# A four-layer graph network that streams its adjacency matrix: six fours in the last upper pair, states turned in couples, four steps moved

## The reference

```python
h = relu(layernorm(x));  x = x + adj @ (h * keep / 0.9)               # layer 0
h = relu(layernorm(x));  deg = clip(rowsum(adj) + 1, 1)               # layer 1
z = concat([h, (adj @ h + h) / deg]) @ W1 + b1
x = x + relu(z) / norm(relu(z))
h = relu(layernorm(x));  a = adj + I;  d = rowsum(a) ** -0.5          # layer 2
x = x + ((d[:, None] * a * d[None, :]) @ h) @ W2
h = relu(layernorm(x))                                                # layer 3
x = x + concat([h, (adj @ h) / (rowsum(adj) + 1)]) @ W3.T
```

## Time and profile before

| | |
|---|---|
| median of 3 runs | 1855.67 us |
| profiled execution | 1858.4 us |
| its span, first to last instruction | 1856.6 us |
| TensorE busy | 1806.5 us (97%) |
| VectorE busy | 1461.4 us (79%) |
| ScalarE, GpSimd busy | 102.1 us, 9.1 us |
| HBM read | 673.3 MB, 365 GB/s over the span |
| mean granted TensorE clock | 0.998 |

### The profile page before, as it was taken

How to read it: one execution, slowest core, us unless ns; L and a number is a source line. 1 busy time by engine, 2 the same in 40 slices (tenths; PEclk the granted TensorE clock), 3 DMA queues, 4 the chain that set the end, 5 groups by cost and what they waited for, 6 DMA issues and landing times.

```text
span 1856.6 us, 21067 instructions
## 1 busy us (share of the span) xinstructions
PE 1806.5 (97%) x8392; PEld 624.2 (34%) x8392; DVE 1461.4 (79%) x1529; ACT 102.1 (6%) x270; POOL 9.1 (0%) x23
## 2 busy tenths in 40 slices
PE   5899999999999999999999999999999999999998
PEld 1223333333333333333333333333333333333333
DVE  8989899999997765669888664678878787877754
ACT  0000000000000000100000000111000000000000
POOL 0000000000000000000000000000000000000000
PEclk9999999999999999999999999999999999999999
DMA  9999999999988878298797798499899999999995
GB/s 384 421 421 421 421 421 421 421 421 421 416 333 319 318 282 298 70 408 329 293 393 317 302 365 333 167 366 420 347 422 374 421 383 421 421 393 421 421 421 236
DMA packets 96047, 676.79 MB, mean 365 GB/s; under 512 B 11216, under 2 KB 13264, under 8 KB 14288
## 3 DMA queue, kind: packets, MB, share of 16 engines
q1 hardware_dynamic: 93024, 673.23, 89.1%
q10 hardware_dynamic: 2928, 2.23, 0.4%
HBM read 673.32 MB, written 2.10 MB: 364 GB/s over the span
## 4 chain that ended last, share of the span: by engine, by line
PE 88%; DMA 7%; DVE 4%; issue 0%; SPq 0%; ACT 0%; DVEq 0%
PE acc L776 43%; DMA ring<-stream_in 7%; PE acc L976 5%; PE acc L950 5%; PE DEG L932 4%; PE acc L806 3%; PE HT L776 2%; PE acc L963 2%; PE Z L832 2%; PE acc L1162 2%; PE DEG L1174 2%; PE acc L1079 2%; PE acc L1055 2%; PE acc L1069 2%; PE acc L1110 1%; PE acc L1117 1%
## 5 line engine op out<-in xcount | busy, mean ns | idle before, releaser
L776 PE MATMUL acc<-ring,states 128*64 128x512 f32 x3984 | 901.7, 595 | 33.7 <-DMA ring<-stream_in 29.1
L776 PEld LDWEIGHTS acc<-ring,states 128*64 128x64 f32 x3984 | 286.8, 137 | 583.3 <-issue 553.3
L1579 DVE TENSOR_TENSOR row_sum<-row_sum,ring 128x2048 f32<-128x2048 f32 x194 | 444.6, 2292 | 14.7 <-DMA ring<-stream_in 9.7
L1703 DVE TENSOR_TENSOR ring<-row_totals,ring 128x2048 f32<-128x2048 f32 x27 | 61.8, 2289 | 56.1 <-PE DEG L934 55.9
L932 PE MATMUL DEG<-ring,states 128*64 128x512 f32 x216 | 99.2, 602 | 3.6 <-DMA ring<-stream_in 3.6
L950 PE MATMUL acc<-row_totals,row_sum 128*64 128x512 f32 x216 | 97.3, 593 | 2.7 <-DVE row_sum L1695 2.7
L934 PE MATMUL DEG<-ring,states 128*64 128x512 f32 x216 | 99.3, 603 | 0.0
L978 PE MATMUL acc<-ring,states 128*64 128x512 f32 x216 | 97.7, 595 | 0.0
L976 PE MATMUL acc<-ring,row_sum 128*64 128x512 f32 x216 | 97.7, 595 | 0.0
L952 PE MATMUL acc<-ring,row_sum 128*64 128x512 f32 x216 | 97.3, 593 | 0.0
L776 PE MATMUL acc<-diag,states 128*64 128x512 f32 x336 | 91.1, 594 | 0.6 <-DMA diag<-stream_in 0.6
(11 more groups left out here) (207 smaller groups left out, 2087.0 us busy)
## 6 DMA issues: line engine op xcount, KB each, us to landing
ring<-stream_in SPq DMA_DIRECT2D x610, 1024.0 KB, 12.5
diag<-stream_in SPq DMA_DIRECT2D x28, 1024.0 KB, 13.2
x<-x_in SPq DMA_DIRECT2D x4, 512.0 KB, 7.0
y<-u_in SPq DMA_DIRECT2D x4, 512.0 KB, 8.9
x_out<-x ACTq DMA_DIRECT2D x16, 128.0 KB, 6.7
below<-w_in ACTq DMA_DIRECT2D x6, 16.0 KB, 5.7
bias<-b_in ACTq DMA_DIRECT2D x1, 32.0 KB, 10.0
```

Source lines behind the costliest of these rows:

```text
L776: return nc.tensor.matmul(half_of(bank, half), h[layer % 2][:, J], moving, start=start, stop=stop)
L1579: nc.vector.tensor_tensor(row_sum[:, :], before, slot(key)[:, :], ALU.add).then_inc(unit_summed, 1 if count > 1 else 2)
```

## The change

1. The last upper pair (2, 1) gets two more fours, on sources (7, 6) and (5, 4), in place of four `plain_both`. Their formed states go into the diagonal slots that the first two couples held.
2. `turn_own` takes several rows: it does their transposes one behind the other, into alternate halves of HT. Rows 14 and 13, and 12 and 11, are turned together; each later pair's two rows are turned right behind the `finish` of the pair before (`close_and_turn`); in the down stage rows b-2 and b-1 behind `finish(c)`, at the end of the pair.
3. Row 15's layer-1 diagonal product, its turn and `finish(1, 15)` come one head step sooner.
4. `cover(15)` goes into the upper head, ahead of `SECOND_D[3]`. `cover(11)` goes from pair 1 to the end, `cover(6)` from the end to pair 4, ahead of `plain` 3. The loads and the let-go order follow.
5. `add_one_again` of the first head diagonal goes ahead of `gather_1(0)`.
6. In the down stage the first sum of each pair's second four is formed sooner (`first_down_form(p, 1)`), behind `end_layer_2(b - 1)`.

```diff
+LAST_SOURCE_PAIRS = [(7, 6), (5, 4)]
 FOURS = [[sp for sp in SOURCE_PAIRS if sp[1] > hi] for hi, lo in PAIRS]
+FOURS[-1] += LAST_SOURCE_PAIRS
+SOURCE_PAIRS += LAST_SOURCE_PAIRS
...
-    [("cover", 15), ("cover", 13), ("four", 0), ("near", 0), ("four", 1), ("plain", 11)],
-    [("cover", 12), ("four", 0), ("four", 1), ("near", 1), ("four", 2), ("cover", 11), ("plain", 9)],
+    [("cover", 13), ("four", 0), ("near", 0), ("four", 1), ("plain", 11)],
+    [("cover", 12), ("four", 0), ("four", 1), ("near", 1), ("four", 2), ("plain", 9)],
...
-    [("cover", 7), ("four", 0), ("four", 1), ("near", 4), ("four", 2), ("four", 3), ("plain", 7), ("plain", 6),
-     ("plain", 5), ("plain", 4), ("plain", 3)],
+    [("cover", 7), ("four", 0), ("four", 1), ("near", 4), ("four", 2), ("four", 3), ("four", 4), ("four", 5),
+     ("cover", 6), ("plain", 3)],
...
-COVER_AT_END = [6, 5, 4, 3, 2, 1]
+COVER_AT_END = [11, 5, 4, 3, 2, 1]
...
-        out += [("sums", p, 0), ("fourth", p, 0), ("turn", 2 * p), ("rest", p, 0)]
-        out += groups(min(p, 2)) + [("turn", 2 * p + 1)] + ([("group", ("own", b - 1))] if p else [])
+        out += [("sums", p, 0), ("fourth", p, 0)] + ([] if p else [("turn", 0, 1)])
+        out += [("rest", p, 0)] + groups(min(p, 2)) + ([("group", ("own", b - 1))] if p else [])
...
-        out += [("rest", p, last), ("near", p)] + groups(1) + [("group", ("near", p)), ("finish", c)]
-    out += groups(1) + [("turn", ROWS - 4)] + groups(1) + [("turn", ROWS - 3)] + groups(len(waiting))
-    return out + [("group", ("own", LAST)), ("turn", ROWS - 2)]
+        out += [("rest", p, last), ("near", p)] + groups(1) + [("group", ("near", p)), ("finish", c), ("turn", b - 2, b - 1)]
+    return out + groups(len(waiting)) + [("group", ("own", LAST))]
...
+            def turn_own(layer, *rows_of_layer):
+                first = TURNS.index((layer, rows_of_layer[0]))
+                if first > 0:
+                    pe.wait_ge(hT_copied, first)
...
+                for n, b in enumerate(rows_of_layer, first):
+                    pe.wait_ge(scaled_ready, n + 1)
+                    for k in range(2):
+                        mm_t = nc.tensor.transpose(turned(n)[:, k * P:(k + 1) * P], scaled[n % 2][:, k * P:(k + 1) * P],
+                                                   ident[:, :])
+                mm_t.then_inc(hT_done, len(rows_of_layer))
...
+            def close_and_turn(p):
+                if p > 0:
+                    finish(1, PAIRS[p - 1][1])
+                turn_own(1, *PAIRS[p])
...
             head_first(2, FIRST_A[1])
-            head_first(2, FIRST_A[2])
             pe.wait_ge(diag_plus_one, ROWS)
...
-            head_first(2, FIRST_C[0], behind=lambda: finish(1, LAST))
+            head_first(2, FIRST_A[2], behind=lambda: finish(1, LAST))
+            head_first(2, FIRST_C[0])
...
             head_second(2, SECOND_D[2], behind=lambda: finish(1, 12))
+            pe.wait_ge(*gathered(1, LAST))
+            cover(LAST)
             head_second(2, SECOND_D[3], behind=lambda: finish(1, 11))
             head_second(2, SECOND_D[4])
-            pe.wait_ge(*gathered(1, LAST))
...
-            end_layer_1(15, lambda: gather_1(14), lambda: gather_1(13))
+            end_layer_1(15, None, lambda: gather_1(14))
+            gather_1(13)
...
+                if len(FOURS[p]) > 4:
+                    for n in range(len(SOURCE_PAIRS) - len(LAST_SOURCE_PAIRS), len(SOURCE_PAIRS)):
+                        form_states(n)
+                    first_form(p, 4)
+                    third_form(p, 4)
+                    last_forms(p, 4)
+                    first_form(p, 5)
+                    third_form(p, 5)
+                    last_forms(p, 5)
                 end_layer_1(before_lo)
...
+            add_one_again(ADDED[0])
             gather_1(0)
-            for r in ADDED[:HEAD]:
+            for r in ADDED[1:HEAD]:
...
                     end_layer_2(b - 1)
+                    first_down_form(p, 1)
                     fold_up_to(GROUPS.index(("own", b - 1)) - 1)
...
+                scale_own(3, b - 2)
+                scale_own(3, b - 1)
                 gather_low_and_parts(p)
```

More of the change, by code:

```diff
@@ L273, in units_let_go @@
         out[at:at + len(ended)] = ended
+        if phase == 2:
+            out.insert(at + 2 * STEPS_AHEAD_OF_COVER, out.pop(at + len(ended)))
     down = down_let_go()
@@ L416, in formed, with turned @@
             at = n % 2 * 4 * FEATS + (t - 1) * FEATS
-            return diag[n // 2][:, at:at + FEATS].rearrange("p (k f) -> p k f", f=F)
+            return diag[n // 2 % 2][:, at:at + FEATS].rearrange("p (k f) -> p k f", f=F)
+        def turned(n):
+            return HT[:, n % 2 * 2 * P:(n % 2 + 1) * 2 * P]
         def down(name):
@@ L616, in copy_hT @@
             def copy_hT(layer, b):
-                act.wait_ge(hT_done, TURNS.index((layer, b)) + 1)
+                n = TURNS.index((layer, b))
+                act.wait_ge(hT_done, n + 1)
                 by_parity = own_y(b, 1).rearrange("p (k l n) -> p l k n", k=2, l=2)
                 for parity in range(2):
-                    turned = HT[parity * F:(parity + 1) * F, 0:2 * P].rearrange("p (k n) -> p k n", k=2)
-                    done = nc.scalar.copy(by_parity[:, parity], turned)
+                    half = turned(n)[parity * F:(parity + 1) * F, :].rearrange("p (k n) -> p k n", k=2)
+                    done = nc.scalar.copy(by_parity[:, parity], half)
                 done.then_inc(hT_copied, 1)
@@ L1045, in cover, with four_even @@
                 both_at_once((2, 0, g), BANK_UP[0], g == LAST, g == 1)
-            def four_even(p, i, after_first=None, after_second=None):
+            def four_even(p, i, after_first=None):
                 (hi, lo), (s1, s2) = PAIRS[p], FOURS[p][i]
@@ L1074, in four_even @@
                 four.then_inc(unit_freed, 1)
-                if after_second is not None:
-                    after_second()
                 pe.wait_ge(unit_formed, 3 * n + 2)
@@ L1224, in _ @@
                         turn_degrees()
-                    if b == LAST and g in (12, 13):
-                        turn_own(1, 26 - g)
+                    if b == LAST and g == 13:
+                        turn_own(1, 14, 13)
                 pe.wait_ge(*diag_arrived(1, b))
@@ L1279, in _ @@
                             pe.wait_ge(part_copied, PARTS.index((2, 11)) + 1)
-                        four_even(p, 0, after_first=(lambda: finish(1, PAIRS[p - 1][1])) if p else None,
-                                  after_second=lambda: turn_own(1, hi))
-                        turn_own(1, lo)
-                    elif kind == "four" and n % 2 == 0:
+                        four_even(p, 0, after_first=lambda: close_and_turn(p))
+                    elif kind == "four" and n == 2:
                         four_even(p, n, after_first=lambda: near_diagonal(p))
@@ L1286, in _ @@
                             turn_own(1, 0)
+                    elif kind == "four" and n % 2 == 0:
+                        four_even(p, n)
                     elif kind == "four":
@@ L1331, in _ @@
                 elif kind == "turn":
-                    turn_own(3, what)
+                    turn_own(3, *step[1:])
                 elif what[0] == "near":
@@ L1677, in early_forms, with third_down_form @@
                 dve.wait_ge(down_formed, 4 * n + 1)
+            def third_down_form(p, i):
+                n = DOWN_BEFORE[p] + i
+                a21, a22, a11, a12 = down_four(p, i)
                 dve.wait_ge(*loaded(a11))
@@ L1681, in early_forms @@
                 dve.wait_ge(down_formed, 4 * n + 2)
+            def early_forms(p, i):
+                first_down_form(p, i)
+                third_down_form(p, i)
             def state_forms(p, i):
@@ L1796, in _ @@
                 end_layer_1(before_hi, begun=True)
-                for n in range(FORMED_BY_GPSIMD, len(SOURCE_PAIRS)):
+                for n in range(FORMED_BY_GPSIMD, len(SOURCE_PAIRS) - len(LAST_SOURCE_PAIRS)):
                     if SOURCE_PAIRS[n][1] == before_hi:
@@ L1832, in _ @@
                     fold_up_to(GROUPS.index(("near", p - 1)) + 1)
-                scale_own(3, 2 * p)
-                scale_own(3, 2 * p + 1)
+                if p == 0:
+                    scale_own(3, 0)
+                    scale_own(3, 1)
                 second_form(p, 0)
@@ L1839, in _ @@
                     end_layer_2(b - 1)
+                    first_down_form(p, 1)
                     fold_up_to(GROUPS.index(("own", b - 1)) - 1)
                 for i in range(1, last):
-                    early_forms(p, i)
+                    if i == 1:
+                        third_down_form(p, i)
+                    else:
+                        early_forms(p, i)
                     state_forms(p, i)
```

32 lines of the change are left out of this document (12 added, 20 removed).

## The result

The kernel after takes 1843.27 us in the median of 4 runs (1842.71 to 1843.66), the kernel before beside it 1855.85 (4 runs): -12.6 us, a ratio of 0.9929 with a 95% interval of 0.9916 to 0.9941. Run once more, with new runs of the kernel before on another occasion, it gave 1843.35 against 1856.35: 0.9927 [0.9914, 0.9939]. The forecast was 1842.3, within 1837.5 to 1848.

The account below looks back on a forecast made before the run. TensorE's order was taken to bound the kernel, except where VectorE's chain or the down stage's full transfers do. Terms -4.05, 0, +0.44, -3.43, -1.75, -2.0 and -2.6 sum to -13.4 us: 1855.67 to 1842.3, range 1837.5 to 1848.

Parts of the forecast that it names:

- terms 1 and 2: Upper head: row 15's couples and the rebuilt step order remove late-state waits and a turn; -4.05 us together.
- (3): Upper pairs 1 to 4: the couples' nominal 2.5 us turns into waits for a VectorE form; 0, bounds -2.5 and 0.
- (4): Upper pairs 1 and 4: covers balance, but `plain` 9 waits for row 9's states without cover 11; +0.44 us.
- (5): Last upper pair: two more fours replace four `plain_both`, one step less; -3.43 us.
- (6): Second head: row 0's half step no longer waits for a diagonal; -1.75 us, lower bound 0.72.
- (7): Down stage, pairs 0 to 5: couples and a sooner second-four sum, capped by transfers in late pairs; -2.0 us.
- (8): Behind the last raw step: coupled turns, an earlier root and folds, and a shorter finish wait; -2.6 us.
- A: Down stage: transfers don't cap, so pairs 3 to 5 give their full 1.92 us; 1836 us, chance 0.13.
- B: New fours, head and diagonal: DVE takes gains back; 1848 us, chance 0.17.
- C: Down pairs 4 and 5: new waits at last raw steps halve the clock, 1.7 us each; 1845.7 with both, chance 0.08.
- D: Last upper pair: DVE's chain falls behind PE, putting all 22.3 us on the path; 1864.6 us, chance 0.05.
- E: Whole kernel: turns' gains hide and waits move, leaving only the new fours' step; 1852.2 us, chance 0.07.

Follow-up runs that it names:

- Experiment 7: Kernel after with row 11's two roots ahead of ScalarE's two copies in the upper head: 1842.33 us.
- experiment 10: Experiment 7's kernel with the first near step's two units asked for behind three units of the second four: 1841.52 us.
- experiment 9: Kernel after with the turns of upper pairs 1 to 4 one row at a time again: 1843.98 us, against 1843.35 for the kernel after.
- Experiment 8: Kernel after with the second form of the second four ahead of the third four's first sum, in upper pairs 1 to 4: 1843.42 us.
- experiment 1: Kernel after without the two new fours, the last upper pair using plain steps 7 to 4 again: 1847.45 us.
- experiment 2: Kernel before with only row 1's diagonal readied ahead of row 0's gathering: 1854.41 us, against 1856.46 for the kernel before.
- Experiment 4: Kernel after with the down stage's turns one row at a time again, each where it was before: 1845.54 us.
- 5 and 6: Half the columns loaded for 63 down-stage units: on the kernel after 1837.71 us, on the kernel before 1855.17 us against 1856.46.
- experiment 3: Kernel before with only the sum of each down pair's second four formed sooner: 1854.98 us, against 1856.46 for the kernel before.

## Why the prediction was right, and where not

**The price of a turn** (terms 1, 3, 7, 8): right. A couple's four transposes last 0.66 us, and behind a finish the next step starts 0.42 later than without them, as in down pairs 2 to 5 (+0.44 at each couple). By itself, in pair 0, it saved 0.31.

**The upper head** (terms 1 and 2): forecast -4.05, measured -3.15. The order of the steps was rebuilt rightly: no wait for states, and the fifth second step ends at 791.05 against 790.8. What failed is the sentence "its chain then ends 2.0 sooner". Before, the two copies started 0.8 us apart, at 792.06 and 792.88, since the two halves of the last second step had come apart in a wait for states. With this wait gone both products end together, both copies are let go at one time, and the root stands behind 1.18 us of copying. So the root came 1.1 us sooner where the step's end came 1.7 sooner. I moved the whole chain by the step's gain and did not ask what the removed wait had kept apart. Experiment 7 shows that this was one half of the miss at most: with the roots ahead of the copies PE kept 0.44 us. Behind it stand the transfers, until experiment 10 asked for the units in the order of their use; the two together give 1.76, more than the miss. The prediction had looked at one transfer there, the first four's last unit, and put it rightly at about 0.7 us (0.53 measured), but not at those behind it.

**Turns in the upper pairs at nothing** (3), **cover 11** (4): right. The waits for VectorE's form are 0.48 us each, `plain` 9 waits 0.32, and experiment 9 shows that in these pairs a saving on TensorE mostly moves the wait: the chain on VectorE from the pair's first finish is what lasts. Experiment 8 shows that the order on that chain isn't neutral: it is worth 0.24 us in each of pairs 2 to 4 and costs 0.87 in pair 1. The weights of L1129 wait longer, as forecast: 5.4 us in four waits of 1.36. The forecast read the old ones wrongly: the 2.3 us of the earlier trace rows are three of the four waits, the fourth stands in a row of its own with `row_totals`, and each is 0.76, not 0.57. The 0.60 that each grew is what the couple saved.

**The two fours** (5): right, -3.43 forecast, 3.42 in the timelines of experiment 1 (4.1 in its runs). VectorE was never behind.

**The diagonal** (6): right, -1.75, and experiment 2 shows it by itself.

**The down stage** (7): right in its sum, -2.0 against -1.88, and in its mechanism. Pairs 0 to 5 gave -0.31, -0.60, -1.35, -0.33, +0.47 and +0.23; forecast were -0.31, -0.62, -1.42, -0.5, +0.42 and +0.42. Experiments 4, 5 and 6 agree from three sides that from pair 3 on the transfers set the pace. Experiment 4 divides the sum in another way than the prediction did: of the couples' own gain nothing is left at pair 5's last raw step, and what term 7 brings is the sooner sum (1.5 us by itself in experiment 3), with 0.3 that no run separates.

**The end** (8): right, -2.53 against -2.6; experiment 4 gives it back as 2.5.

**The rivals.** A (transfers don't cap) is out by experiments 4 to 6. B had a point in the head alone. C: the waits it needs are there (1.69 and 1.73 us), its half clock is not. D fell with experiment 1, E with the result. (The chances of the forecast, A, B and C add up to 0.88, so "faster by more" with a little of E was more than the 0.87 given.)

**What agreed by luck:** the sum. The head gave 1.0 less than forecast, and the down stage's first step, for which the prediction had no term, some 0.6 to 1.4 more; the two nearly cancel. The spans of the two profiles differ by 14.8 us, as before's had its half clock and its latest transfer. That this execution was 2.7 us over the median was written down, and the difference could be carried over, since no term was taken from that stretch. Had the gain been read off the two spans, it would have come out some 2 us too large.

## What to carry to other kernels

A record's wait isn't its price: a part of a side-by-side step runs alone ahead of it, so 0.72 us cost 1.75; and a wait removed lets things go together that it had kept apart, so follow each of them to the in-order queue behind it. Before counting a gain, find the next anchor behind it: where the transfers run at their full rate from a slot let go to the step that waits, what is gained between is lost at that step, while what is gained ahead of the first slot or behind the last wait is kept. And where a ring lies full and then opens, the order of asking should be that of use to the unit, since everything comes at one fixed distance.

## What was unexpected of the hardware

The granted clock's last fall comes at the end of every profile, around the 2.49 us wait ahead of the last finish, but not at one place: this finish lasted 1.10 us in the profiles of before and of experiments 7, 9 and 10, where the clock fell 1.0 to 1.6 us behind its start, and 1.97 in both of the kernel after, where it fell 1.1 to 1.3 us ahead of it. It is up to 0.87 us of difference for the same work, and the wait is the same in all. That it also differs between executions of one program is likely but not shown by a profile: of the four timed runs of after, those with a mean granted clock of 0.999 have spans of 1840.8 and 1841.1 us, those with 0.998 have 1841.7 and 1841.8. Of the four profiles with a wait of 1.51 to 2.40 us at the down stage's first step only the one with 2.40 went to half clock, from 1208.38 to 1211.80 us; in eight of the thirteen profiles the clock was still full when the wait of 2.49 us at the end was over.

A transfer asked for when the DMA engines were idle landed 4.8 us later (787.76 to 792.60 in after; others 4.7 to 5.6), the ones behind it 2.49 us apart, with single gaps of 2.8 to 4.3. Some of these gaps are no accident of an execution: in the two profiles of after three of the longest end at 1243.1, 1249.4 and 1330.1 us, and at 1243.4, 1249.9 and 1330.1. Where one falls on a unit that TensorE waits for, as on the second of the down stage in the kernels made from before, it counts in every execution that was profiled.
